# Scattering the expert results into the output by accumulation, with the shared part stored ahead or behind

## The chip, the cores and the metric

The kernel runs on one core of a Trainium2 chip. The metric is the device time of one launch in microseconds (us), the median of several runs. Profiles are of one execution; times in them count from the start of its span.

## The reference

The model takes 64 sequences of 64 points with 7 channels. After a signature layer and an attention layer, the last layer is a mixture of experts over all tokens (4096 in the kernel, 32 tiles of 128, 128 features each). What matters here is how the output comes together from three terms:

```python
h = _L0_tok_ref(x, L0_tok_W, L0_tok_b)
h = h + _L0_attn_ref(_layernorm(h), ...)
h = h + _L0_ffn_ref(_layernorm(h), ...)

# _L0_ffn_ref, with E = 8 experts, K = 1 chosen per token, I = 512 hidden
logits = xf @ gate_w.T
wts, idx = jax.lax.top_k(logits, K)
wts = jax.nn.softmax(wts, axis=-1)          # 1.0, since K = 1
h = silu(xf @ w1[e].T) * (xf @ w3[e].T)     # e: the token's expert
y = h @ w2[e].T
y = y + gelu(xf @ sw1.T) @ sw2.T            # the shared part, for all tokens
```

So out = residual + shared part + the part of the token's one expert.

## The kernel before, in words

Tokens lie in 32 tiles; `h` in SBUF holds the residual of all 32 (128 partitions x 32 x 128, 2 MB). A first stage, to about 510 us, loops over the tiles and makes the residual, the normalised rows `x2` and the router's logits; GpSimd scatters the rows of `x2`, with their token number behind them, into `sorted_rows` in DRAM, in order of expert and padded to slabs of 128 (L502).

The shared part is computed in eight groups of four tiles (`GROUPS` = 8, `AHEAD` = 6). SyncE loads a group's columns (`load_group`, L377), ScalarE and VectorE split them in two parts for an exact product (`xg_hi`, `xg_lo`, L709 and L796), TensorE does `up` and `down`, ScalarE the gelu between (L714), and VectorE adds the result to `h` (`add_shared`, L1152, counted by the semaphore `added`). Groups 0 to 5 are done ahead of the experts. Groups 6 and 7 have their up products behind the last slab and their down products at the very end, in PSUM banks 5, 6 and 1, so that TensorE has work while the last transfers land.

Between them run the experts: `SORTED` = 39 slabs. For each slab j, with k = j mod 2, SyncE reads the slab's first row number from `row_i` and loads 128 rows (`load_rows`, L413), when slab j-2 has been transposed and its token numbers kept (`rT_psum`, `id_kept`); TensorE transposes the rows (L1556) and does the two up products, ScalarE silu (L739), VectorE the product of the two (L1204), the copy of the expert's weights (L1190) and the copy of the token numbers (L1199), TensorE the down product, ScalarE copies the result to `y[k]` (L750), and GpSimd scatters `y[k]` to `expert_rows` in DRAM by token number (L573); rows of padding carry a number out of range and are skipped. The copy to `y[k]` waits until the scatter of slab j-2 has landed (`y_sent`).

Behind the experts, SyncE waits for all scatters, reads `expert_rows` back in eight transfers of 256 KB (L432, groups 6 and 7 first), VectorE adds each to `h` (L1233), then adds the last shared results from PSUM to groups 6 and 7 in three pieces (`add_last_shared`, L1239), and SyncE stores the output in nine transfers as the pieces are finished (L437). Each engine's work stands in one program in order; each waits on semaphores counted. SyncE's queue carries all plain transfers, GpSimd's the scatters.

Of the kernel before, what the change touches and what calls it, by code (L numbers as in the profile page):

```python
# [30 lines left out]
F32 = mybir.dt.float32  # L31
# [4 lines left out]
ALU = mybir.AluOpType  # L36
# [3 lines left out]
P = 128  # L40
SEQS, LEN, CHANNELS = 64, 64, 8
TILES = SEQS * LEN // P
DIM = 128
# [22 lines left out]
GROUP = 4  # L66
# [25 lines left out]
def build(nc, x_next, x_prev, w_low, w_high, tok_b, wqkv, u_qkv, wout_t, u_columns, b_out,  # L92
          scalars, gate_t, w13_t, w2_t, sw1_t, sw2_t, square, mask_c, steps, out):
    with ExitStack() as ctx:
# [3 lines left out]
        def sem(name):  # L98
            return ctx.enter_context(nc.semaphore(name))

        x2T_dram = nc.dram_tensor("x2_columns", [P, TILES * P], F32, kind="Internal").ap()
        sorted_rows = nc.dram_tensor("sorted_rows", [SLABS * P, ROW], F32, kind="Internal").ap()
        expert_rows = nc.dram_tensor("expert_rows", [TILES * P, DIM], F32, kind="Internal").ap()

# [163 lines left out]
        rowsT = late(2, P)  # L268
        expert_in = x2[:].rearrange("p t r -> p (t r)")[:, 0:TILES * DIM].rearrange("p (t d) -> p t d", d=DIM)
        w13_tile = x2[:].rearrange("p t r -> p (t r)")[:, 0:4 * HIDDEN].rearrange("p (k i) -> p k i", k=2)  # L270
# [46 lines left out]
        xg_loaded = [sem(f"x_group_loaded{n}") for n in range(2)]  # L317
        expert_loaded = [sem(f"expert_rows_loaded{n}") for n in range(GROUPS)]
        expert_added, finished, out_sent = sem("expert_rows_added"), sem("finished"), sem("out_sent")
        rows_in = [sem(f"rows_in{n}") for n in range(2)]  # L320
# [12 lines left out]
        def _(sp):  # L333
# [42 lines left out]
            def load_group(g):  # L376
                sp.dma_start(xg_in[:, g % 2, :], x2T_dram[:, g * GROUP * P:(g + 1) * GROUP * P]) \  # L377
                    .then_inc(xg_loaded[g % 2], 16)
# [31 lines left out]
            def load_rows(j, k):  # L410

                row = sp.value_load(row_i[0:1, bass.ds(j, 1)], min_val=0, max_val=(SLABS - 1) * P)
                sp.dma_start(rows[:, k, :], sorted_rows[bass.ds(row, P), :]).then_inc(rows_in[k], 16)  # L413

            for g in range(GROUPS - 4):
                sp.wait_ge(xg_lo, g + 3)
                load_group(g + 4)
            sp.wait_ge(pos_ready, 4)
            sp.wait_ge(scattered, 16 * TILES)
            for j in range(2):  # L420
                load_rows(j, j)
            with sp.Fori(2, SORTED - 2, 2) as j:
                for k in range(2):
                    sp.wait_ge(rT_psum, j + (k - 1))
                    sp.wait_ge(id_kept, j + (k - 1))
                    load_rows(j + k, k)
# [3 lines left out]

            def load_experts(g):
                sp.dma_start(expert_in[:, g * GROUP:(g + 1) * GROUP, :],  # L432
                             expert_rows[g * GROUP * P:(g + 1) * GROUP * P, :].rearrange("(t p) d -> p t d", p=P)) \
                    .then_inc(expert_loaded[g], 16)

            def store(first, tiles):
                sp.dma_start(out[first * P:(first + tiles) * P, :].rearrange("(t p) d -> p t d", p=P),  # L437
                             h[:, first:first + tiles, :]).then_inc(out_sent, 16)

            for k in range(2):  # L440
                sp.wait_ge(y_sent[k], 16 * ((SORTED + 1 - k) // 2))
            for g in (AHEAD, AHEAD + 1, *range(AHEAD)):
                load_experts(g)
            for g in range(GROUPS - 1):
                sp.wait_ge(finished, g + 1)
                store(g * GROUP, GROUP)
            for n in range(2):
                sp.wait_ge(finished, GROUPS + n)
                store((GROUPS - 1) * GROUP + 2 * n, 2)
            sp.wait_ge(out_sent, 16 * (GROUPS + 1))  # L450


        @block.gpsimd
        def _(pool):
# [114 lines left out]
            scatter(range(EARLY, TILES))  # L569

            for j in range(SORTED):
                pool.wait_ge(y_done, j + 1)
                nc.gpsimd.indirect_dma_start(  # L573
                    out=expert_rows[:, :], out_offset=bass.IndirectOffsetOnAxis(ap=ids[:, j:j + 1], axis=0),
                    in_=y[:, 2 if j == SORTED - 1 else j % 2, :], in_offset=None, bounds_check=TILES * P - 1, oob_is_err=False) \
                    .then_inc(y_sent[j % 2], 16)

# [202 lines left out]
        def _(d):  # L780
# [448 lines left out]

            def add_experts(g):  # L1230
                d.wait_ge(expert_loaded[g], 16)
                hg = tiles_of(h, g * GROUP, GROUP)
                return V.tensor_tensor(hg, hg, tiles_of(expert_in, g * GROUP, GROUP), ALU.add)  # L1233

            def add_last_shared(n, tiles, bank, done):

                d.wait_ge(down_psum, done)
                hg = tiles_of(h, AHEAD * GROUP + n, tiles)
                V.tensor_tensor(hg, hg, B[bank][:, 0:tiles * DIM], ALU.add).then_inc(finished, 1)  # L1239

            for g in (AHEAD, AHEAD + 1):
                add_experts(g).then_inc(expert_added, 1)
            for g in range(AHEAD):
                add_experts(g).then_inc(finished, 1)
            d.wait_ge(expert_added, 2)
            add_last_shared(0, GROUP, 5, AHEAD + 1)
            add_last_shared(GROUP, 2, 6, AHEAD + 2)
            add_last_shared(GROUP + 2, 2, 1, AHEAD + 3)


# [460 lines left out]
```

## Time and profile before

| | before |
|---|---|
| median of 3 runs | 676.93 us (676.33 to 677.5) |
| the profiled execution | 676.65 us |
| its span | 674.8 us |
| TensorE busy | 638.4 us (95%) |
| VectorE, ScalarE, GpSimd busy | 417.5, 288.2, 298.7 us |
| DMA moved | 61.81 MB, 92 GB/s mean |
| DMA in the last of 40 slices | 250 GB/s |

The span runs from the first to the last instruction that the profile shows. A row of the timeline gives start and duration in us, engine, line, operation, output and input; what stands in brackets is the idle time of the engine ahead of it and what ended it. Names are those of the memory and not always of the view: `prob` stands for `y`, `xvo` for the slab's rows, `x` for the copied expert weights or the reloaded rows, `levels` for w2, `sw` for the shared weights, `tail`, `z`, `xqk` and `xvp` for the gelu's results. SPq rows are transfers issued by SyncE, with the time that the issue took; "to landing" counts from the start of the issue to the completion.

### The profile page before, as it was taken

To read this page: it belongs to the slowest core of one execution; us is meant where nothing else is said; L and a number is where in the kernel's file an instruction comes from. 1 tells how busy PE (TensorE), PEld (TensorE's weight loads), DVE (VectorE), ACT (ScalarE), POOL (GpSimd) and SP (SyncE) were. 2 spreads that over 40 slices of the span, in tenths; PEclk is the share of its full clock that TensorE was granted. 3 is DMA by queue.
4 is the path that set the end of the run, shared out by engine and by line. 5 is a ranking of instruction groups with operands and counts; after the bars stand their busy time and mean duration, and the time that the engine had idled before them with its cause. 6 is when DMAs were issued, how large, how long until landed. Compare 5 with 4: busy or idle time off the path is not lost.

```text
span 674.8 us, 14377 instructions
## 1 busy us (share of the span) xinstructions
PE 638.4 (95%) x4237; PEld 539.0 (80%) x4270; DVE 417.5 (62%) x1073; ACT 288.2 (43%) x656; POOL 298.7 (44%) x336
## 2 busy tenths in 40 slices
PE   5989999999999999999999999999798999999994
PEld 3767888877888788887788887778577999999994
DVE  7966666666666666665666667776535354555534
ACT  3334444544445444445444454433374433444450
POOL 1355444545445454455444454445853213333330
PEclk9989999999999999999999999999988999999997
DMA  8511433534634434334343342112335211111108
GB/s 310 220 68 33 106 78 85 116 80 101 118 78 111 92 87 101 78 92 111 78 105 82 79 114 46 36 35 69 86 91 191 64 33 38 43 44 44 46 26 250
DMA packets 70006, 61.81 MB, mean 92 GB/s; under 512 B 6092, under 2 KB 58189, under 8 KB 69600
## 3 DMA queue, kind: packets, MB, share of 16 engines
q1 hardware_dynamic: 67712, 57.31, 33.6%
q0 software_dynamic: 2272, 4.22, 1.8%
q8 instruction: 13, 0.21, 0.1%
q14 instruction: 9, 0.07, 0.0%
HBM read 18.88 MB, written 26.30 MB: 67 GB/s over the span
## 4 chain that ended last, share of the span: by engine, by line
PE 81%; DVE 7%; issue 4%; POOL 3%; ACT 2%; DMA 1%; SPq 1%; DVEq 0%; POOLq 0%; ACTq 0%
PE bank L1256 74%; PE bank L1312 2%; PE bank L1465 2%; POOL sorted_rows L502 1%; POOL z L487 1%; DMA x<-expert_rows 1%; SPq L432 1%; PE bank L1556 1%; PE bank L1371 1%; PE bank L1362 0%; PE bank L1317 0%; POOL z L489 0%; PE bank L1316 0%; DMA sq<-square 0%; DVE utl L796 0%
## 5 line engine op out<-in xcount | busy, mean ns | idle before, releaser
L1256 PE MATMUL bank<-whigh,uth 128*128 128x512 f32 x512 | 168.8, 410 | 1.2 <-DVE lowt L796 1.2
L1256 PEld LDWEIGHTS bank<-whigh,uth 128*128 128x128 f32 x512 | 92.2, 190 | 28.0 <-issue 7.4
L1256 PE MATMUL bank<-whigh,utl 128*128 128x512 f32 x256 | 101.8, 398 | 0.0
L496 POOL TENSOR_TENSOR rstd<-rstd,powers 128x1 f32<-128x1 f32 x64 | 35.3, 551 | 119.9 <-DVE rstd L889 64.7
L487 POOL TENSOR_TENSOR z<-z 128x512 f32<-128x512 f32 x32 | 42.3, 1322 | 91.0 <-DVE z L902 91.0
L573 POOL DMA_INDIRECT expert_rows<-prob,ids x39 | 38.3, 983 | 89.2 <-ACT prob L750 89.2
L1256 PE MATMUL bank<-xvo,x 128*128 128x128 f32 x624 | 76.4, 276 | 0.7 <-issue 0.4
L1256 PEld LDWEIGHTS bank<-xvo,x 128*128 128x128 f32 x624 | 72.8, 192 | 1.4 <-issue 0.7
L1256 PE MATMUL bank<-xT,qkw 128*128 128x128 f32 x512 | 63.7, 278 | 0.0
L1256 PEld LDWEIGHTS bank<-xT,qkw 128*128 128x128 f32 x512 | 60.8, 195 | 0.1
L1256 PEld LDWEIGHTS bank<-whigh,utl 128*128 128x128 f32 x256 | 48.3, 189 | 11.9
L902 DVE TENSOR_TENSOR z<-bank,v 128x512 f32<-128x512 f32 x64 | 44.2, 691 | 20.6 <-PE bank L1256 16.8
L1204 DVE TENSOR_TENSOR z<-tail,bank 128x512 f32<-128x512 f32 x39 | 26.8, 688 | 48.3 <-PE bank L1256 48.3
L641 ACT ACTIVATE prob<-prob 128x512 f32<-128x512 f32 x32 | 20.2, 633 | 66.4 <-DVE prob L1020 63.6
L623 ACT ACTIVATE xqk<-bank,fac 128x512 f32<-128x512 f32 x64 | 43.9, 690 | 7.2 <-PE bank L1256 5.7
L651 ACT COPY pt<-bank 128x512 f32<-128x512 f32 x32 | 18.8, 587 | 63.8 <-PE bank L1465 61.7
L1256 PEld LDWEIGHTS bank<-xvp,pt 128*64 128x64 f32 x512 | 30.1, 137 | 18.2 <-issue 18.2
L482 POOL TENSOR_TENSOR e3l<-e,e3h 128x512 fp32r<-128x512 f32 x31 | 40.4, 1304 | 7.8 <-DVE xn L923 6.5
L1256 PE MATMUL bank<-vow,xTh 128*128 128x512 f32 x128 | 43.1, 418 | 0.0
L911 DVE TENSOR_TENSOR h<-bank,tokb 128x128 f32<-128x128 f32 x32 | 9.3, 291 | 54.2 <-PE bank L1256 54.2
L1256 PE MATMUL bank<-xqk,xT 128*64 128x512 f32 x128 | 34.5, 618 | 8.5 <-DVE logits L957 4.2
L630 ACT COPY xvo<-bank 128x512 f32<-128x512 f32 x64 | 37.6, 587 | 10.6 <-PE bank L1256 8.9
(229 smaller groups left out, 1325.9 us busy)
## 6 DMA issues: line engine op xcount, KB each, us to landing
sorted_rows<-blank SPq DMA_DIRECT2D x24, 709.5 KB, 6.3
xvp<-xvo SPq DMA_DIRECT2D x128, 128.0 KB
w<-w_t SPq DMA_DIRECT2D x1, 4096.0 KB, 12.0
xvo<-sorted_rows SPq DMA_DIRECT2D x39, 64.5 KB, 1.9
w<-w_high SPq DMA_DIRECT2D x4, 512.0 KB, 6.8
x_columns<-x2t SPq DMA_DIRECT2D x32, 64.0 KB
xg_in<-x_columns SPq DMA_DIRECT2D x8, 256.0 KB
levels<-w_t SPq DMA_DIRECT2D x1, 2048.0 KB, 7.7
```

Source lines behind the costliest of these rows:

```text
L482: G.tensor_tensor(e3l[:], e3[:], e3h[:].bitcast(F32), ALU.subtract).then_inc(e3_lo, 1)
L487: G.tensor_tensor(z4[:], z[:, 0:4, :], z[:, 4:8, :], ALU.add).then_inc(tree, 1)
L496: G.tensor_tensor(rstd[:, n, 1:2], rstd[:, n, 0:1], powers[:, 0:1], ALU.pow) \
L573: nc.gpsimd.indirect_dma_start(out=expert_rows[:, :], out_offset=bass.IndirectOffsetOnAxis(ap=ids[:, j:j + 1], axis=0), in_=y[:, 2 if j == ...
L623: A.activation(xqk[:, :, 4 * n:4 * n + 4, :], B[5 + n][:].rearrange("p (s h k) -> p s h k", s=2, h=4), ACT.Copy, scale=fac[:, 1:2]).then_i ...
L630: A.copy(xvo[:, n, :, :].rearrange("p c d -> p (c d)"), B[7 - 2 * n][:]) \
L641: A.activation(prob[:], prob[:], ACT.Exp).then_inc(exp_done, 1)
L651: A.copy(pt[:].rearrange("k c s q -> k (c s q)"), B[6][:]).then_inc(pT_sb, 1)
L902: V.tensor_tensor(z[:, cs, :], B[1 + half][:].rearrange("p (c d) -> p c d", c=4), spread(v[:, bass.ds(s, 1), cs].rearrange("p o c -> p (o ...
L1204: V.tensor_tensor(hidT[:, k, :, :].rearrange("p c t -> p (c t)"), act[:, k, :], B[2 + 2 * k][:], ALU.mult).then_inc(hid_done, 1)
L1256: return T.matmul(out_, lhsT, rhs, start=start, stop=stop)
L1312: T.transpose(B[0][:, col(c)], u4[:, col(c)], ident)
```

## The change

The tensor `expert_rows` is gone. GpSimd's 39 scatters go to `out` itself and add to what is there (`compute_op=ALU.add`). For that the rest of the output must be there first: SyncE stores the residual of groups 6 and 7 when it is complete (`h2_done`), and each of groups 0 to 5 when its shared part has been added, all counted by `out_begun`, between the loads of the columns (L377) and between the first row loads (L413). GpSimd waits for all eight before its first scatter. Behind the experts only groups 6 and 7 are read back, as sums of residual and expert part; VectorE adds the last shared results to these in three pieces and writes `h`, and SyncE stores the three pieces.

```diff
-        expert_rows = nc.dram_tensor("expert_rows", [TILES * P, DIM], F32, kind="Internal").ap()
...
+            def out_tiles(first, tiles):
+                return out[first * P:(first + tiles) * P, :].rearrange("(t p) d -> p t d", p=P)
+
+            def store(first, tiles, done):
+                sp.dma_start(out_tiles(first, tiles), h[:, first:first + tiles, :]).then_inc(done, 16)
+
+            sp.wait_ge(h2_done, TILES)
+            for g in range(AHEAD, GROUPS):
+                store(g * GROUP, GROUP, out_begun)
             for g in range(GROUPS - 4):
                 sp.wait_ge(xg_lo, g + 3)
                 load_group(g + 4)
+                sp.wait_ge(added, g + 1)
+                store(g * GROUP, GROUP, out_begun)
             sp.wait_ge(pos_ready, 4)
             sp.wait_ge(scattered, 16 * TILES)
             for j in range(2):
                 load_rows(j, j)
-            with sp.Fori(2, SORTED - 2, 2) as j:
+            sp.wait_ge(added, AHEAD - 1)
+            store((AHEAD - 2) * GROUP, GROUP, out_begun)
+            for j in range(2, 4):
+                sp.wait_ge(rT_psum, j - 1)
+                sp.wait_ge(id_kept, j - 1)
+                load_rows(j, j % 2)
+            sp.wait_ge(added, AHEAD)
+            store((AHEAD - 1) * GROUP, GROUP, out_begun)
+            with sp.Fori(4, SORTED - 2, 2) as j:
...
             for k in range(2):
                 sp.wait_ge(y_sent[k], 16 * ((SORTED + 1 - k) // 2))
-            for g in (AHEAD, AHEAD + 1, *range(AHEAD)):
-                load_experts(g)
-            for g in range(GROUPS - 1):
-                sp.wait_ge(finished, g + 1)
-                store(g * GROUP, GROUP)
             for n in range(2):
-                sp.wait_ge(finished, GROUPS + n)
-                store((GROUPS - 1) * GROUP + 2 * n, 2)
-            sp.wait_ge(out_sent, 16 * (GROUPS + 1))
+                sp.dma_start(sums_in[:, n * GROUP:(n + 1) * GROUP, :], out_tiles((AHEAD + n) * GROUP, GROUP)) \
+                    .then_inc(sums_loaded[n], 16)
+            sp.wait_ge(finished, 1)
+            store(AHEAD * GROUP, GROUP, out_sent)
+            for n in range(2):
+                sp.wait_ge(finished, 2 + n)
+                store((GROUPS - 1) * GROUP + 2 * n, 2, out_sent)
+            sp.wait_ge(out_sent, 16 * 3)
...
+            pool.wait_ge(out_begun, 16 * GROUPS)
             for j in range(SORTED):
                 pool.wait_ge(y_done, j + 1)
                 nc.gpsimd.indirect_dma_start(
-                    out=expert_rows[:, :], out_offset=bass.IndirectOffsetOnAxis(ap=ids[:, j:j + 1], axis=0),
-                    in_=y[:, 2 if j == SORTED - 1 else j % 2, :], in_offset=None, bounds_check=TILES * P - 1, oob_is_err=False) \
-                    .then_inc(y_sent[j % 2], 16)
+                    out=out[:, :], out_offset=bass.IndirectOffsetOnAxis(ap=ids[:, j:j + 1], axis=0),
+                    in_=y[:, 2 if j == SORTED - 1 else j % 2, :], in_offset=None, bounds_check=TILES * P - 1, oob_is_err=False,
+                    compute_op=ALU.add).then_inc(y_sent[j % 2], 16)
...
-            def add_experts(g):
-                d.wait_ge(expert_loaded[g], 16)
-                hg = tiles_of(h, g * GROUP, GROUP)
-                return V.tensor_tensor(hg, hg, tiles_of(expert_in, g * GROUP, GROUP), ALU.add)
-
             def add_last_shared(n, tiles, bank, done):
 
                 d.wait_ge(down_psum, done)
-                hg = tiles_of(h, AHEAD * GROUP + n, tiles)
-                V.tensor_tensor(hg, hg, B[bank][:, 0:tiles * DIM], ALU.add).then_inc(finished, 1)
-
-            for g in (AHEAD, AHEAD + 1):
-                add_experts(g).then_inc(expert_added, 1)
-            for g in range(AHEAD):
-                add_experts(g).then_inc(finished, 1)
-            d.wait_ge(expert_added, 2)
+                V.tensor_tensor(tiles_of(h, AHEAD * GROUP + n, tiles), tiles_of(sums_in, n, tiles),
+                                B[bank][:, 0:tiles * DIM], ALU.add).then_inc(finished, 1)
+
+            d.wait_ge(sums_loaded[0], 16)
             add_last_shared(0, GROUP, 5, AHEAD + 1)
+            d.wait_ge(sums_loaded[1], 16)
             add_last_shared(GROUP, 2, 6, AHEAD + 2)
             add_last_shared(GROUP + 2, 2, 1, AHEAD + 3)
```

## Rows read from the trace of the kernel before

**Rows 1.** Chain of work that ended last, 640 to 675 us: start, us, what

```profile
656.11 2.11 DMA expert_rows<-prob,ids
658.23 0.39 SPq L432
...
663.37 4.94 DMA x<-expert_rows
```

**Rows 2.** Timeline of the tail: TensorE, VectorE, SyncE

```profile
661.08 0.69 DVE L1233 TENSOR_TENSOR h<-h,x 128x512 f32<-128x512 f32 x1 [8.71 <-DMA x<-expert_rows]
...
661.89 0.61 PE L1256 MATMUL bank<-sw,z 128*128 128x128 f32 x4
...
665.46 0.61 PE L1256 MATMUL bank<-sw,xvp 128*128 128x128 f32 x4
...
669.87 0.41 DVE L1239 TENSOR_TENSOR h<-h,bank 128x256 f32<-128x256 f32 x1
...
670.71 0.59 SPq L437 DMA_DIRECT2D out<-h  x1
```

**Rows 3.** Landing of the nine output stores (L437), and SyncE's end (L94)

```profile
DMA to landing us min/median/max: 3.1/3.2/3.7
...
L94 SPq COMPARE_BRANCH  x1: 38/38/38, 674.4 to 674.4; - x1
```

**Rows 4.** Landing of the 39 scatters of expert results (L573)

```profile
DMA to landing us min/median/max: 2.1/2.6/3.4
```

**Rows 5.** DMA issues: kind, count, KB each, median us to landing (a slab's row load)

```profile
xvo<-sorted_rows SPq DMA_DIRECT2D x39, 64.5 KB, 1.9
```

**Rows 6.** Timeline of 505 to 550 us, SyncE, ScalarE, VectorE, TensorE and GpSimd

```profile
509.64 0.34 SPq L374 DMA_DIRECT2D x_columns<-x2t  x1
510.02 0.43 SPq L407 DMA_DIRECT2D levels<-w_t  x1
511.20 0.34 SPq L377 DMA_DIRECT2D xg_in<-x_columns  x1
...
518.33 0.62 ACT L709 CAST uth<-xg_in 128x512 fp32r<-128x512 f32 x1 [2.10 <-DMA xg_in<-x_columns]
520.52 1.29 ACT L714 ACTIVATE xqk<-bank 128x512 f32<-128x512 f32 x2 [1.57 <-PE bank L1256]
...
525.91 0.48 PE L1256 MATMUL bank<-uth,sw 128*128 128x512 f32 x1
...
528.78 0.60 PE L1256 MATMUL bank<-sw,xqk 128*128 128x128 f32 x4
...
529.49 0.69 DVE L1152 TENSOR_TENSOR h<-h,bank 128x512 f32 x1 [3.78 <-remote]
...
531.94 0.35 SPq L413 DMA_DIRECT2D xvo<-sorted_rows  x1
...
533.07 0.35 SPq L413 DMA_DIRECT2D xvo<-sorted_rows  x1
...
533.57 0.68 DVE L1152 TENSOR_TENSOR h<-h,bank 128x512 f32 x1
...
538.71 0.38 PE L1556 MATMUL bank<-sq,xvo 128*128 128x128 f32 x2
...
541.17 2.05 PE L1256 MATMUL bank<-xvo,x 128*128 128x128 f32 x16 [0.29 <-DVE x L1190]
...
545.05 0.69 DVE L1152 TENSOR_TENSOR h<-h,bank 128x512 f32<-128x512 f32 x1 [0.26 <-PE bank L1256]
...
548.89 1.00 POOL L573 DMA_INDIRECT expert_rows<-prob,ids  x1 [19.38 <-ACT prob L750]
```

**Rows 7.** Timeline of two slabs in the steady state: ScalarE's result, GpSimd's scatter

```profile
635.89 0.27 ACT L750 COPY prob<-bank 128x128 f32<-128x128 f32 x1 [0.63 <-PE bank L1256]
...
636.92 0.98 POOL L573 DMA_INDIRECT expert_rows<-prob,ids  x1 [1.73 <-ACT prob L750]
...
641.46 0.27 ACT L750 COPY prob<-bank 128x128 f32<-128x128 f32 x1 [0.62 <-PE bank L1256]
```

## What I predict, and from what

> **What bounds the kernel now.** I read the chain of waits first, since a change behind the experts pays only where that chain runs, then the timeline of the last 20 us by engine, then the landings of the transfers, and last the stretch from 505 to 550 us, where the moved stores go. Through the router, the shared groups and the 39 expert slabs the chain is TensorE's. It leaves TensorE at the last slab: the last scatter is issued at 656.11 and lands 2.11 us later, SyncE issues eight reloads of the expert rows from 658.23, the last of them at 663.37, and that one counts as landed 4.94 us later [rows 1]. Only then can VectorE finish: the adds of the last shared groups end at 669.87 + 0.41 = 670.28, SyncE issues the last store at 670.71, and it has landed when SyncE goes on at 674.4 [rows 2, 3]. TensorE had finished the last product that these adds need at 665.46 + 0.61 = 666.07 [rows 2]. So 4.2 us of VectorE's last add, and more behind it, are owed to 2 MB of reloads and 2 MB of stores, not to arithmetic. The reader is to see in rows 1 and 2 that the end is a transfer chain laid over a TensorE chain that ends 4 us earlier.
>
> **Tail, the gain.** The change takes out six of the eight reloads, the eight adds of 128x512, and six of the nine stores there. What is left I follow from the last scatter.
> The scatter is now an accumulation: each row of 512 B of the output is read, added to and written. No row of before shows one. It can't be quicker than a plain scatter, since the same bytes still travel the same way: 2.1 us at least, 2.6 median, 3.4 at most [rows 4]. The dear end is a read followed by a plain scatter, one after the other: 1.9 (a slab's row load, [rows 5]) + 2.6 = 4.5 us. I take 3.2, nearer the plain scatter, because the 64 KB are the same, and the read may overlap within the transfer.
> Landing at 656.11 + 3.2 = 659.3; reload of group 6 issued at 659.4 and landed 2.85 us later, as the first of the eight was (issued 658.23, add begun 661.08, [rows 1, 2]): 662.2. TensorE ends group 6 at 661.89 + 0.61 = 662.5 [rows 2], so the reload is already covered. Group 7's reload is issued half a us later and is there at some 663.2, while its second half comes from TensorE at 666.07. Even with the dear 4.5 us it is there at 664.6. So the accumulation's price in the tail is nothing; it would show from a landing of about 6 us on.
> VectorE's last add then starts right behind TensorE and takes 0.41: 666.1 + 0.4 = 666.5; SyncE issues the store of 128 KB at 666.6. Its landing: the nine stores of before took 3.1 to 3.7 us [rows 3], with up to eight others in the queue. The other bound is the last spill of 64 KB in the same 512 B rows: issued at 509.64, and SyncE was past the wait for it when it issued the load at 511.20, so at most 1.56 us [rows 6]. With one store of 128 KB two us ahead of it the last one is alone; I take 2.6, between the ends. It lands at 669.2, and 674.8 - 674.4 = 0.4 us of ending follow: span 669.6, a gain of 5.2. With 1.56 it is 668.6, with 3.7 it is 670.7.
> [...]
>
> **Expert stage, where the accumulation can cost.** ScalarE writes y of slab j only when slab j-2's scatter has landed. In the steady state the result is copied at 635.89 for 0.27 us, its scatter starts at 636.92, and the copy two slabs on is at 641.46 [rows 7]. So a scatter may take 641.46 - 636.92 = 4.54 us before ScalarE waits; the plain one took 3.4 at most. Above 4.5 the loop of two slabs (5.57 us) is paced by the landing, and with 37 slabs behind it each us more costs 18.5 us. At 3.2 it costs nothing: TensorE's 2.8 us a slab cover it. The dear end from the rows, 4.5, lies just at the edge. GpSimd's own instruction, 0.98 us in a slab of 2.79, may take up to 2.5 us before it binds. More descriptors should lengthen it somewhat; I count nothing.
> The Trainium skill (Collectives: The Full Stack, The bandwidth ceiling) says that a reducing transfer is slowed by its second source read and not by the add, and measures about half the rate of a copy. No run here shows that yet. It would leave a scatter of 64 KB far under the 4.5 us and the sum as it is.
>
> **Stores moved ahead.** SyncE gets eight stores of 256 KB, at 0.38 us of issue each, and three kinds of neighbours.
> First, groups 6 and 7 are stored before the load of columns of group 4, which was issued at 511.20 behind the 2 MB load of w2 [rows 6]. That load had ScalarE wait until 518.33. Two issues are 0.8 us and 512 KB in the queue; at the 284 GB/s at which the 2.36 MB before that point passed (510.02 to 518.33) they are 1.8 us, so the columns are there at 520.2 and copied at 520.8. ScalarE's next gelus, which started at 520.52, start 0.3 us late; TensorE wants their product only in the down product that starts at 528.78 [rows 6]. Cost nothing.
> Second, the loads of groups 5 to 7 now stand behind a wait for the previous group's add as well. The last of these, group 3's add, runs at 533.57 + 0.68 = 534.25 [rows 6]. Behind it on SyncE are a store (0.4) and the first two row loads, which were issued at 531.94 and 533.07. With 0.8 us to read the row number they go out at 535.5 and 536.6, 3.6 us later, and land at 537.4 and 538.5 by the median 1.9 [rows 5, 6]. TensorE transposes them at 538.71 [rows 6]. That is on the edge: with the largest neighbouring landing, 3.7, TensorE would wait 1.7 us, of which 0.29 are slack before the first expert product at 541.17 [rows 6]. I take 0.1 us.
> Third, stores of groups 4 and 5. The first goes out at about 539.8, before the next row load. The second goes out when VectorE's add at 545.05 is done, 545.8, and lands by 549.5 at the latest. GpSimd now waits for all eight stores before its first scatter; that was at 548.89 [rows 6]. Likely nothing, at most 0.7 us + 0.5 of preparation, and the second scatter at 551.7 absorbs it. This wait is right by the Trainium skill (DMA: Bandwidth & Descriptors, Rules for kernel authors): a plain write beside an accumulation of the same bytes is lost; no run here shows that.
> Sum: 674.8 - 5.2 + 0.1 = 669.7 us of span, a run of 676.65 - 5.1 = 671.55 in the profiled execution's own count. The median of the three runs is 0.28 above the profiled one, so 671.8.
>
> **Rivals.**
> (a) The accumulation paces the experts: slower. Its landing decides, from 4.5 us on. At 4.54 + 5.1 / 18.5 = 4.82 the whole gain is gone; at 5.5 the kernel takes 671.8 + 18.5 x 0.96 = 690 us, at 6 us 699. For it: no row of an accumulation exists, and eight rows per engine with a read before each write need not overlap as well as plain writes. Against it: even a serial read and write come to 4.5. Chance 0.15 for slower (above 678.3), 0.04 for the narrow band of no change (675.6 to 678.3).
> (b) The moved transfers hold up TensorE between 510 and 550: row loads landing late (up to 1.4 us, above), and a code fetch. For the latter: VectorE stood 3.78 us until 529.49 for something that the profile calls remote, though the product it needed was done when TensorE began the next group at 525.91, 0.3 us of overlap aside [rows 6]. If that is code coming through the same DMA engines, 512 KB of stores before it add up to 2 us, and only the part of it beyond TensorE's own lead is lost. Together 1 to 3 us of the gain go: 672.8 to 674.8. Chance 0.14.
> (c) The change doesn't shorten the tail by as much, since the last store lands as slowly as now (3.7) and no less: 672.9 at most; that is the upper end of my own forecast and no sign of its own. Against more: TensorE's end at 666.07 is untouched.
> (d) A quicker end, with a lone store of 1.6 us or less: 670.7. Part of the forecast, its outer edge (below 670.4) 0.05.
>
> **How the numbers follow.** Forecast with its edges (670.4 to 672.9): 0.62; (b) 0.14; (d) beyond the edge 0.05; (a) 0.15 slower and 0.04 same. The likeliest time is 671.8. The range must hold 8 in 10: from 670.4 to 675.0 holds 0.76, so I reach into the narrow band about no change, to 677.0, which holds 0.80. About 0.2% (1.35 us) is what a measurement of this kernel can tell from none. Faster 0.81, same 0.04, slower 0.15.
>
> **What would show it.** After: the scatter's landing (right if 2.6 to 4.5 and ScalarE nowhere waits for one; the loop stays at 2.79 us a slab); TensorE's last product still 10 to 11 us behind the last scatter's issue; VectorE's last add within 0.5 us of it; only two reloads; the last store's landing 1.6 to 3.1 and not 3.7; the first two row loads at 535.5 and 536.6 and no wait of TensorE before 538.7; the first scatter near 549. A slab period above 2.9 us would prove (a), a shift of the first expert product with an unchanged period (b).

## The result and the profile after

The changed kernel takes 670.04 us (median of four runs, 669.5 to 671.37), the kernel before 676.63 beside it: a ratio of 0.9905 with a 95% interval of 0.9886 to 0.9925, so 5 to 8 us less. In a second set it took 669.38 us against 676.4, ratio 0.989 (0.9873 to 0.9907). The forecast was 671.8 and its range began at 670.4: the direction and the place were right, the size was too small, and the first median fell 0.4 us below the range.

The profiled execution has a span of 668.4 us (670.26 us as a run). First its page: GpSimd's busy time has grown by 22.5 us, and each of its scatters from 0.98 to 1.56 us, while TensorE's busy time is nearly what it was (638.4 and 637.1 us).

```profile
span 668.4 us, 14362 instructions
PE 637.1 (95%) x4237; PEld 538.7 (81%) x4270; DVE 411.8 (62%) x1065; ACT 289.3 (43%) x656; POOL 321.2 (48%) x336
L583 POOL DMA_INDIRECT out<-prob,ids x39 | 60.9, 1560 | 65.9 <-ACT prob L760 65.9
```

The end of its chain of waits (start, us, what) answers [rows 1]. The transfers have left the chain: TensorE runs without a stop to the last product, then comes one add.

```profile
648.57 17.22 PE bank L1258 x128
665.78 0.02 issue
665.81 0.42 DVE h L1243
```

The timeline of the tail answers [rows 2 and 3]: last scatter, two reloads (658.51 and half a us later), TensorE's last product, the three adds, the last store, and the moment when SyncE has seen it land.

```profile
655.78 1.56 POOL L583 DMA_INDIRECT out<-prob,ids  x1 [1.00 <-ACT prob L760]
...
658.51 0.94 SPq L452 DMA_DIRECT2D x<-out  x2
...
662.30 0.69 DVE L1243 TENSOR_TENSOR h<-x,bank 128x512 f32<-128x512 f32 x1 [10.26 <-PE bank L1258]
...
664.09 0.42 DVE L1243 TENSOR_TENSOR h<-x,bank 128x256 f32<-128x256 f32 x1 [1.10 <-PE bank L1258]
...
665.16 0.61 PE L1258 MATMUL bank<-sw,xvp 128*128 128x128 f32 x4
665.81 0.42 DVE L1243 TENSOR_TENSOR h<-x,bank 128x256 f32<-128x256 f32 x1 [1.29 <-PE bank L1258]
...
666.25 0.37 SPq L418 DMA_DIRECT2D out<-h  x1
...
L94 SPq COMPARE_BRANCH  x1: 38/38/38, 668.0 to 668.0; - x1
```

All three adds are released by TensorE and none by a reload, as the brackets say. The last product ends at 665.16 + 0.61 = 665.77, so 2.6 us are left behind TensorE (8.7 before: 674.8 - 666.07). The list of transfers (count, KB each, median us to landing) shows what the sum had as guesses: an accumulating scatter lands in 3.3 us, a store of 128 KB in 1.8, and the two reloads take 3.0 and 4.3 (3.7 is their median). The last scatter was quicker than the others: SyncE, which waits for it, issued the reloads 658.51 - 655.78 = 2.73 us after its start.

```profile
out<-prob,ids POOLq DMA_INDIRECT x39, 3.3
...
x<-out SPq DMA_DIRECT2D x2, 256.0 KB, 3.7
...
out<-h SPq DMA_DIRECT2D x2, 128.0 KB, 1.8
```

In the stretch ahead of the experts, answering [rows 6], the first shared up product of group 2 started at 512.07 instead of 510.99. By that much the executions differ before they reach anything that was changed. All later times are therefore to be read from that point.

```profile
520.95 0.62 ACT L719 CAST uth<-xg_in 128x512 fp32r<-128x512 f32 x1 [3.60 <-DMA xg_in<-x_columns]
521.62 1.29 ACT L724 ACTIVATE xqk<-bank 128x512 f32<-128x512 f32 x2
...
527.41 0.69 DVE L1162 TENSOR_TENSOR h<-h,bank 128x512 f32 x1 [0.60 <-PE bank L1258]
...
536.00 1.51 SPq L412 DMA_DIRECT2D xvo<-sorted_rows  x2
...
540.62 0.68 PE L1258 MATMUL bank<-sw,xqk 128*128 128x128 f32 x4 [0.43 <-issue]
...
542.48 1.95 PE L1258 MATMUL bank<-xvo,x 128*128 128x128 f32 x16
...
550.17 1.61 POOL L583 DMA_INDIRECT out<-prob,ids  x1 [19.55 <-ACT prob L760]
```

### The profile page after: what moved, and what is told of

Its sections match the earlier page's. It is cut to its first block, busy times and chain, and to the rows that moved or that the text cites. A ratio compares the mean times of both kernels' runs of the same rounds, so it can differ in the third digit from the quotient of the medians.

```text
span 668.4 us, 14362 instructions
## 1 busy us (share of the span) xinstructions
PE 637.1 (95%) x4237; PEld 538.7 (81%) x4270; DVE 411.8 (62%) x1065; ACT 289.3 (43%) x656; POOL 321.2 (48%) x336
## 3 DMA queue, kind: packets, MB, share of 16 engines
q0 software_dynamic: 6640, 4.22, 4.6%
## 4 chain that ended last, share of the span: by engine, by line
PE 84%; DVE 6%; POOL 5%; issue 3%; ACT 1%; DMA 0%; SPq 0%; ACTq 0%; DVEq 0%; POOLq 0%
PE bank L1258 78%; POOL sorted_rows L511 3%; PE bank L1314 2%; PE bank L1467 2%; POOL z L496 1%; PE bank L1558 1%; POOL rstd L505 1%; PE bank L1373 1%; PE bank L1364 1%; PE bank L1319 0%; POOL z L498 0%; PE bank L1318 0%; DMA sq<-square 0%; DVE utl L806 0%; DVE whigh L806 0%
## 5 line engine op out<-in xcount | busy, mean ns | idle before, releaser
L583 POOL DMA_INDIRECT out<-prob,ids x39 | 60.9, 1560 | 65.9 <-ACT prob L760 65.9
## 6 DMA issues: line engine op xcount, KB each, us to landing
xvo<-sorted_rows SPq DMA_DIRECT2D x39, 64.5 KB, 1.8
```

What stands on the lines that cost most here:

```text
L583: nc.gpsimd.indirect_dma_start(out=out[:, :], out_offset=bass.IndirectOffsetOnAxis(ap=ids[:, j:j + 1], axis=0), in_=y[:, 2 if j == SORTED ...
```

## The experiments

I read three stretches in every profile, since the executions differ by up to 3 us before the first changed instruction: (A) from the first up product of shared group 2 to the first expert product, (B) from there to the end of TensorE's last product, (C) from there to the end of the span. Each is a difference of two times in the timeline, as for the kernel after: 542.48 - 512.07 = 30.41, 665.77 - 542.48 = 123.29, 668.4 - 665.77 = 2.63. What is left, the start up to group 2, is nothing of the change's. The two kernels with one buffer, whose slab loop runs at another pace, are not in the table.

| kernel | A | B | C | stops in slabs 6 and 10 |
|---|---|---|---|---|
| before | 30.18 | 124.90 | 8.73 | 1.24 |
| before, second profile | 30.21 | 125.05 | 8.45 | 1.35 |
| before, third | 30.17 | 125.38 | 8.57 | 1.79 |
| before, fourth | 30.00 | 124.36 | 8.48 | 0.68 |
| before + early stores | 30.56 | 124.38 | 8.96 | 0.90 |
| the same, second profile | 30.38 | 125.22 | 8.78 | 1.63 |
| the same, third | 30.32 | 124.37 | 8.46 | 0.86 |
| plain scatter, no early stores | 30.24 | 124.15 | 2.62 | 0.58 |
| the same, second profile | 30.01 | 124.28 | 2.66 | 0.54 |
| after | 30.41 | 123.29 | 2.63 | 0.00 |
| after, second profile | 30.37 | 123.51 | 2.65 | 0.00 |
| plain scatter | 30.40 | 123.70 | 2.71 | 0.00 |
| reload all | 30.38 | 123.55 | 9.49 | 0.00 |
| small last piece | 30.41 | 124.16 | 2.34 | 0.69 |
| the same, second profile | 30.37 | 123.31 | 2.30 | 0.00 |
| late reload | 28.98 | 123.42 | 3.55 | 0.13 |

The last column is how far the distances between VectorE's products of slabs 6 and 7 and of slabs 10 and 11 exceed the usual 2.79 us, in sum.

**Plain scatter.** Is the accumulation covered?

```diff
-                    in_=y[:, 2 if j == SORTED - 1 else j % 2, :], in_offset=None, bounds_check=TILES * P - 1, oob_is_err=False,
-                    compute_op=ALU.add).then_inc(y_sent[j % 2], 16)
+                    in_=y[:, 2 if j == SORTED - 1 else j % 2, :], in_offset=None, bounds_check=TILES * P - 1, oob_is_err=False).then_inc(y_sent[j % 2], 16)
```

> The changed kernel with the 39 scatters as plain writes (the output lacks the shared part and residual where an expert row overwrote it). My theory: the accumulation is hidden behind TensorE, so the time is that of the changed kernel, 670.0 us, within 0.5; the scatter lands in 2.6 us instead of 3.3 and GpSimd's instruction falls from 1.56 to 0.98 us. The rival, that the longer scatter costs something in the slab loop, expects 1 to 3 us less than the changed kernel and a shorter slab period than 2.79.

669.49 us, ratio 0.9908 (0.9889 to 0.9926), no different from the changed kernel. Its scatters land in 2.5 us and take GpSimd 0.98:

```profile
L583 POOL DMA_INDIRECT out<-prob,ids x39: 982/982/1002, 548.4 to 654.4; - x39
DMA to landing us min/median/max: 2.1/2.5/4.2
```

So accumulation adds 0.8 us to the median landing, 0.58 of it GpSimd's own work on the instruction, and in this kernel it costs nothing that the times show.

**No early stores.** What do the moved stores cost? All eight and GpSimd's wait are left out, on top of the plain scatter.

```diff
-            sp.wait_ge(h2_done, TILES)
-            for g in range(AHEAD, GROUPS):
-                store(g * GROUP, GROUP, out_begun)
...
-                sp.wait_ge(added, g + 1)
-                store(g * GROUP, GROUP, out_begun)
...
-            pool.wait_ge(out_begun, 16 * GROUPS)
```

> As the plain scatter, and with the eight stores ahead of the experts and GpSimd's wait for them left out (the output holds the expert part alone in groups 0 to 5). My theory: the stores cost TensorE 0.1 to 0.3 us between 510 and 541 us, so this is within 0.4 us of the plain scatter, about 669.8. The rival, that the moved stores hold up the stretch before the experts, expects 1 to 2 us less, 668 to 669, with the first up product of the shared groups and the first expert product earlier.

669.86 us, ratio 0.9914 (0.9893 to 0.9934): no difference. Stretch A puts the stores at 0.2 to 0.3 us: 30.0 to 30.2 in the six profiles without them, 30.3 to 30.6 in nine with them (in the tenth, the late reload's, TensorE's first products of group 2 took 0.50 instead of 0.80 us, and the granted clock was 1.00 (2.4 GHz) from 511 to 513 us where the changed kernel had 0.50 (1.2 GHz), so A can't be compared). With the stores TensorE pauses 0.40 to 0.61 us behind the transposition of the first rows in the five profiles read for it (0.43 in the row at 540.62 above); without them it pauses there not at all and 0.30 before the first expert product, for VectorE's copy of the weights:

```profile
541.63 2.05 PE L1247 MATMUL bank<-xvo,x 128*128 128x128 f32 x16 [0.30 <-DVE x L1189]
```

The rival that the moved transfers cost 1 to 3 us is out.

**Reload all.** Is the whole gain in the tail? The changed kernel with all eight groups reloaded, added and stored behind the experts, in the order of before.

```diff
-            for n in range(2):
-                sp.dma_start(sums_in[:, n * GROUP:(n + 1) * GROUP, :], out_tiles((AHEAD + n) * GROUP, GROUP)) \
-                    .then_inc(sums_loaded[n], 16)
+            for g in (AHEAD, AHEAD + 1, *range(AHEAD)):
+                sp.dma_start(sums_in[:, g * GROUP:(g + 1) * GROUP, :], out_tiles(g * GROUP, GROUP)) \
+                    .then_inc(sums_loaded[g], 16)
...
+            for g in (AHEAD, AHEAD + 1):
+                add_experts(g).then_inc(expert_added, 1)
+            for g in range(AHEAD):
+                add_experts(g).then_inc(finished, 1)
```

> The changed kernel up to the last scatter, with the tail of the kernel before: eight reloads, eight adds, nine stores (the shared part is counted twice). My theory: the whole gain is in the tail, so this takes what the kernel before takes, 676.6 us within 0.7, with 8.5 to 9 us from TensorE's last product to the end, and stores that land in 3.1 to 3.7 us. The rival, that 1.6 us of the gain lie in the slab loop, expects 675.0 and a slab stage of 123.3 us from the first expert product to TensorE's end, as against 124.9 in the kernel before.

675.22 us, ratio 0.9989 (0.9976 to 1.0003). Putting the old tail back gives back all but at most 1.6 us of the gain. Stretch C is 9.5 us and the stores wait in the queue again: the seven of 256 KB at the end take 2.8 to 3.6 us, the two of 128 KB 2.8 and 3.7 (1.8 in the changed kernel). The 15 stores of the first row are these seven and the eight early ones.

```profile
out<-h SPq DMA_DIRECT2D x15, 256.0 KB, 3.3
...
x<-out SPq DMA_DIRECT2D x8, 256.0 KB, 4.8
...
out<-h SPq DMA_DIRECT2D x2, 128.0 KB, 3.3
```

But stretch B is 123.55 here. So B is not something that the tail's transfers did; the expectation's rival (675.0 us, B 123.3) was right.

**One buffer.** What is a landing worth once it is on the path? ScalarE's result goes to one buffer instead of two, so it waits for the scatter of the slab just before. The same edit in both kernels:

```diff
-                    in_=y[:, 2 if j == SORTED - 1 else j % 2, :], in_offset=None, bounds_check=TILES * P - 1, oob_is_err=False,
+                    in_=y[:, 2 if j == SORTED - 1 else 0, :], in_offset=None, bounds_check=TILES * P - 1, oob_is_err=False,
...
-                if reused:
-                    a.wait_ge(y_sent[k], (j - k) * 8)
-                nc.scalar.copy(y[:, 2 if is_tile(j, SORTED - 1) else k, :], B[5 + k][:, 0:DIM]).then_inc(y_done, 1)
+                if not is_tile(j, 0) and not is_tile(j, SORTED - 1):
+                    a.wait_ge(y_sent[1 - k], (j + k) * 8)
+                nc.scalar.copy(y[:, 2 if is_tile(j, SORTED - 1) else 0, :], B[5 + k][:, 0:DIM]).then_inc(y_done, 1)
```

> The changed kernel with one buffer for the expert result instead of two, so that ScalarE waits for the scatter of the slab just before. It measures what a landing costs once it paces the loop. My theory: a slab then takes copy 0.27 + 0.77 to the scatter's start + landing 3.3 + 0.05 = 4.4 us instead of 2.79, in 36 slabs 58 us more, 728 us in all. The rival, that a landing on the path is quicker or slower than in the covered loop (fewer transfers beside it, or rows that don't overlap), expects a slab period off 4.4 by 0.5 us or more.

> The kernel before with one buffer for the expert result, against the same edit of the changed kernel. My theory: the plain scatter's landing (2.6 us in the covered loop) paces the loop: 0.27 + 0.77 + 2.6 + 0.05 = 3.7 us a slab, 33 us more than before, 709 us. The difference to the other kernel, 0.7 us a slab, is then what accumulation costs where nothing covers it. The rival, that the uncovered costs are alike, expects a period of 4.3.

The changed kernel takes 727.53 us with it, the kernel before 693.07 (one run each; the difference is far above the spread of 2 us). ScalarE's rows of the first and then of the second show two results, each released by a scatter's landing:

```profile
601.87 0.27 ACT L760 COPY prob<-bank 128x128 f32<-128x128 f32 x1 [3.41 <-DMA out<-prob,ids]
...
606.27 0.27 ACT L760 COPY prob<-bank 128x128 f32<-128x128 f32 x1 [3.48 <-DMA out<-prob,ids]
```

```profile
602.15 0.27 ACT L750 COPY prob<-bank 128x128 f32<-128x128 f32 x1 [2.38 <-DMA expert_rows<-prob,ids]
...
605.45 0.27 ACT L750 COPY prob<-bank 128x128 f32<-128x128 f32 x1 [2.24 <-DMA expert_rows<-prob,ids]
```

A slab takes 4.40 and 3.30 us. The formula of the prediction (copy 0.27, 0.77 to the scatter's start, the landing, 0.05) holds with the landings of these runs: 3.4 gives 4.5, and 2.2 gives 3.3. My expected 3.7 for the plain one was wrong because I took the landing of the covered loop, 2.6. Part of that is the load of a slab's rows: in the covered loop one was under way beside 35 of the 39 plain scatters, which landed in 2.6 at the median, and the last four, with none, landed in 2.1; with one buffer only 4 of the 39 plain scatters had a load beside the part behind GpSimd's, and 30 of the accumulating ones. So uncovered, the accumulating version costs 1.1 us more per slab, but not all of that is shown to be the accumulation. With no row load beside them the last three accumulating scatters of the changed kernel landed in 2.7, 0.6 later than the plain ones, which is what GpSimd's instruction is longer by.

The two buffers and TensorE's 2.79 us per slab are what makes it free, and the margin was thinner than the median says. Two of ScalarE's results are put down to a landing just at the limit of 4.54 us, the first of them this one:

```profile
555.74 1.56 POOL L583 DMA_INDIRECT out<-prob,ids  x1 [1.26 <-ACT prob L760]
...
560.27 0.27 ACT L760 COPY prob<-bank 128x128 f32<-128x128 f32 x1 [0.70 <-DMA out<-prob,ids]
```

From the start of this scatter to ScalarE's copy two slabs on are 4.53 us, and 4.57 for the other (566.89 to 571.46). By the events in the trace three of the 39 scatters landed in 4.3 to 4.5 us, and each had a 16 KB transfer of the queue that the page calls `instruction` beside it (below). The view's own maximum of 3.4 leaves them out, because it has a landing for 19 of the 39 only. TensorE lost nothing by them: the slabs stay at 2.79 us.

**Late reload.** How much cover is left in the tail? The reloads are issued only when TensorE has ended group 6's down product.

```diff
+            sp.wait_ge(down_psum, AHEAD + 1)
             for n in range(2):
```

> The changed kernel with the reloads of groups 6 and 7 issued only when TensorE has ended group 6's down product, 3.7 us later than now. It measures how much of the reload TensorE covers. My theory: group 7's reload, 4.3 us to landing, then comes 1.2 us behind TensorE's last product, and two adds of 0.42 follow instead of one: 4.3 to 4.5 us from TensorE's end to the end of the span instead of 2.6, so 1.8 us more. The rival, that a reload with a quiet queue lands in 2.9 us, expects only 0.4 us more.

669.12 us, ratio 0.9897 (0.9879 to 0.9915): the runs can't tell it from the changed kernel, but stretch C grew from 2.6 to 3.55 us. The three adds now stand in a row behind the reload and no longer behind TensorE, whose last product ended at 662.95:

```profile
662.41 1.55 DVE L1244 TENSOR_TENSOR h<-x,bank 128x512 f32<-128x512 f32 x3 [13.19 <-DMA x<-out]
```

The issue was 3.5 us ahead of TensorE's end, as against 7.3 in the changed kernel. The reloads landed in 2.9 and 3.3 us, where 3.0 and 4.3 were measured in the changed kernel, so group 7's was there 0.2 us behind TensorE and not 1.2. The result, 0.9 us more, lies between theory (1.8) and rival (0.4). It also shows the cover: 3.8 us of delay cost 0.9, so a landing of the last scatter up to some 3 us later would have cost nothing.

**Small last piece.** Can what is left be cut? The last piece of two tiles becomes two of one, the last in a bank of its own.

```diff
-            last_down(AHEAD + 1, 1, range(2, GROUP), 1)
+            last_down(AHEAD + 1, 1, range(2, GROUP - 1), 1)
+            last_down(AHEAD + 1, 1, range(GROUP - 1, GROUP), 2)
...
-            add_last_shared(GROUP + 2, 2, 1, AHEAD + 3)
+            add_last_shared(GROUP + 2, 1, 1, AHEAD + 3)
+            add_last_shared(GROUP + 3, 1, 2, AHEAD + 4)
```

> The changed kernel with its last piece of two tiles cut in two of one tile, the last in a PSUM bank of its own: one add and one store more. What is left behind TensorE is add, store issue, landing and end, 2.6 us. My theory: the add shrinks from 0.42 to 0.28 and the 64 KB land in 1.6 instead of 1.8, so 0.3 us less, 669.7. The rival, that the additional issue on the store queue is late and takes it back, expects no difference or 0.3 us more.

> The changed kernel, unchanged, beside the kernel before and the next one on one chip. My theory: 6.0 us less than the kernel before (5.5 to 6.6), of which 6.1 are the tail and -0.2 the stores ahead. From its first shared up product to its first expert product 30.4 us, as against 30.2 without the stores; from TensorE's end to the end of the span 2.6.

> The version with a last piece of one tile, beside the changed kernel on one chip. Its profile had 2.34 us behind TensorE's end, as against 2.63. My theory: 0.3 us less than the changed kernel. The rival: no difference that five rounds can show.

Both of its profiles have 2.3 us behind TensorE instead of 2.6, as the smaller add (0.29 for 0.42) and the quicker landing (1.5 for 1.8) say. The times are 669.51 and 669.83, the changed kernel's beside the second 669.38, ratio 0.9896 (0.9877 to 0.9914) against 0.989. 0.3 us is below what these runs resolve; the version isn't shown to be faster. The changed kernel itself missed its second expectation: 7.0 us less than the kernel before it, where 5.5 to 6.6 were expected. The tail and the stores were as expected; the rest is stretch B.

**Where 1.5 us of stretch B went.** The kernel before, and the kernel before with the eight early stores alone (groups stored again at the end; the places of the later ones are as in the change):

```diff
+            sp.wait_ge(h2_done, TILES)
+            for g in range(AHEAD, GROUPS):
+                early_store(g * GROUP, GROUP)
             for g in range(GROUPS - 4):
                 sp.wait_ge(xg_lo, g + 3)
                 load_group(g + 4)
+                sp.wait_ge(added, g + 1)
+                early_store(g * GROUP, GROUP)
...
```

> The kernel before, unchanged, profiled once more. In the first profile it took 124.9 us from the first expert product to TensorE's end; five profiles of kernels with the same slab loop took 123.3 to 124.2. My theory: this part varies by about a us from execution to execution (short stops of TensorE, mostly at the ends of the unrolled loop) and the change has no part in it, so a second profile of the kernel before gives 123.3 to 124.9, more likely below 124.5. The rival, that the change itself shortens the slab loop by 1 us or more, expects 124.9 again.

> The kernel before with one part of the change alone: the eight stores ahead of the experts, at the changed kernel's places on the queue (the output is stored again at the end, as before). Open is why TensorE needs 124.9 and 125.1 us from the first expert product to its end in two profiles of the kernel before, and 123.3 to 123.6 in four of six with the stores. The difference lies in two slabs of the first pass of the unrolled loop, the sixth and the tenth (3.1 to 3.8 us instead of 2.79). Theory one, the stores on the queue (and the row loads written out between them) remove those stops: 123.3 to 123.8 us here, 0.2 more ahead, 1.0 less in all than the kernel before. Theory two, it is the new scatter or the shorter program behind the loop: 124.9 us here, and 0.2 us more than the kernel before in all.

> A second profile of the kernel with plain scatters and without the eight stores, whose first one had 3.07 and 3.09 us in the sixth and the tenth slab. If the stores remove the stops, it has both again, 0.5 to 1.3 us together. If the stops are chance, it may have none. From the first shared up product to the first expert product it takes 30.2 us, unless TensorE's clock comes up sooner.

> The kernel before once more, for the stops in the sixth and the tenth slab (so far 1.2 and 1.3 us together). If the stops belong to a program without the stores, 0.5 to 1.4 us again; if they are chance, it may have none.

> The kernel before with the eight early stores alone, once more. Its first profile had no stop in the sixth slab and 0.9 us in the tenth. Theory one, the stores remove stops: 0 to 0.9 us, on average 0.3, and the time 0.3 to 0.8 us below the kernel before. Theory two, chance: the same stops as the kernel before on average, and the time 0.2 us above.

> The kernel before once more, as the third. Timed against itself it is to show no difference, within 0.1%.

> As the kernel before with the eight early stores alone, a third profile, the same expectations.

The kernel before had B at 124.4 to 125.4 in four profiles, the changed one at 123.3 and 123.5. My expectation for the second profile of before (at most 124.9) missed: it was 125.05. Timed against itself, the kernel before gives ratios of 0.9995 (0.9986 to 1.0003) and 0.9997 (0.9985 to 1.001). The kernel with the early stores alone has 124.4, 125.2 and 124.4, and takes 675.77, 675.77 and 675.45 us, ratios 0.9992 (0.9982 to 1.0001), 0.999 (0.9978 to 1.0003) and 0.9997 (0.9984 to 1.0011): the stores alone don't remove the stops, and they don't cost anything that can be measured either. The stops stand in the first pass of the unrolled slab loop; later pauses are 0.2 us at most. In the chain of waits of the kernel before they look like this: a transposition takes 0.20 us in the chain instead of 0.11, and 24 products take 3.24 us instead of 2.68, with a gap of 0.19 for nothing that the profile shows.

```profile
557.95 0.20 PE bank L1556
558.15 1.03 PE bank L1256 x8
559.18 0.19 issue
559.38 2.02 PE bank L1256 x16
```

In the same slab of the second profile of before the idle time is put down to a late row load ahead of the transposition:

```profile
559.01 0.14 PEld L1556 LDWEIGHTS bank<-sq,xvo 128*128 128x128 f32 x1 [0.33 <-DMA xvo<-sorted_rows]
```

That row load is the cause. It was issued at 555.04 in the kernel before and at 556.19 in the changed one, and these are the times to its landing, the first for before and the second for after:

```profile
DMA to landing us min/median/max: 2.7/2.7/2.7
...
DMA to landing us min/median/max: 1.9/1.9/1.9
```

What made it late is in the trace too. The page counts a queue of its own for instructions, and the trace holds its packets:

```profile
q8 instruction: 13, 0.21, 0.1%
```

One of these 13 transfers of 16 KB ran from 555.45 to 556.67. Of the 128 packets of the row load 120 had ended by 556.55, and the last eight ended behind it, up to 557.20. The two loads in question (for the seventh and the eleventh slab), in all 16 profiles of the table, divide without an exception:

| 16 KB instruction transfer starts after the load's issue by | load lands in | stop | cases |
|---|---|---|---|
| 0.1 to 1.0 us | 2.2 to 3.1 us | 0.13 to 1.01 us | 18 |
| 1.3 to 2.2 us | 1.7 to 1.9 us | none | 14 |

A stop is as long as the landing exceeds some 2.1 us. So the stops are instruction transfers that fall on a row load. In the two profiles of the changed kernel they came later and fell on a scatter instead, which the two buffers cover. What sets their time stays open. It isn't the accumulation alone: the plain scatter has no such stops, and without the early stores it has them again, 0.58 and 0.54 us (the latter run took 669.94). So neither the stores alone nor the new scatter alone takes them away, and in the small last piece they came once and not the other time. They depend on the program, and within one program on the execution, so a gain in B is not one to count on.

## Why the prediction was right, and where not

The direction and the mechanism came out as forecast. Two terms of the sum failed, both too dear: the landing of the last store (2.6 us, measured 1.8), and the slab loop, whose change was put at nothing without a look at its first pass (measured 1.6 us less in the profile, 1.5 over all profiles).

- **The place of the gain: right.** The end was a chain of transfers laid over a TensorE chain that ended earlier. Now TensorE's last product releases the last add, and putting the old tail back takes the gain back.
- **Accumulation in the tail and in the slabs: right.** Landing 3.2 forecast, 3.3 measured at the median and 2.7 for the last, and covered: of ScalarE's 39 results two have their idle time (0.70 and 0.73 us) put down to a landing, which is at most 0.03 more than the 0.70 that it stands for TensorE in every second slab anyway. The dear end of 4.5 was reached three times (4.3 to 4.5), not by a serial read and write but beside an instruction transfer; rival (a) was nearer than the median says. The pace formula behind rival (a) was confirmed to 0.1 us by the one-buffer kernels; its condition didn't occur.
- **GpSimd's instruction: counted at no change, grew by 0.58 us.** It lies in 1.7 us of idle time per slab and costs nothing.
- **Reload: mis-sized, covered all the same.** 2.85 forecast, 3.0 to 4.3 measured. Group 6's was there at 661.5, 0.7 us before TensorE ended its product at 662.20, and the bracket of the first add names TensorE. Group 7's was there at 663.3, 2.5 us before TensorE's end, so by my estimate the accumulation would have shown in the tail from a landing of 2.7 + 2.5 = 5.2 us on, and not of 6.
- **Last store: the term that was mis-sized.** 2.6 forecast, 1.8 measured. I went to the middle between a queued store (3.1 to 3.7) and a spill of 64 KB alone (1.56), though by my own sum the last store was alone. The nearer row was the spill. With an add 0.04 us behind TensorE, stretch C came to 2.6 instead of the 3.5 forecast: 0.9 us.
- **Stores moved ahead: 0.1 forecast, 0.2 measured.** Read from the same start (1.08 us off all times), the columns of group 4 came at 519.9, where 520.2 was forecast. The first row load went out at 534.9, where 535.5 was forecast, and the first scatter at 549.1, as forecast.
- **VectorE's unexplained wait of 3.78 us** was not there in the changed kernel (0.60 behind TensorE at 527.41), and in the three other profiles of before it is 0.61 to 0.62 as well. So it was no property of the stretch, and rival (b) had nothing to add to. What it was stays open. Code did come beside the data transfers, as (b) supposed, but where it cost something it delayed row loads in the slab loop, in the kernel before more than in the changed one.
- **Missing from the sum: the stops of stretch B,** 1.24 us in the profile of before and none in the changed one. No step of mine looked at the slab loop's period over all slabs; I took the steady 2.79 us as the whole of it. In the kernel before two row loads of the first pass landed late beside instruction transfers (2.7 us each instead of 1.8 to 1.9); in the changed kernel none did. That was luck for the change as far as is known, and no merit of it.

Forecast 669.7, measured 668.4 in the profile: -0.9 in the tail, +0.1 ahead, +1.1 before anything changed, -1.6 in B, which makes -1.3. Over all profiles the change is worth 5.9 us in the tail (8.56 mean to 2.64), 0.2 us ahead the other way, and 1.5 us in B (124.9 mean to 123.4), 7.2 in sum, for measured medians that differ by 6.6 and 7.0 us. The 0.4 us by which the time fell out of the range are thus the store's landing and B together: the tail alone (0.9 us) would have left it inside, B alone (1.5) at its edge, which lay 1.4 below the forecast. Two small slips of the working changed nothing: by its own rows group 7's reload is there at 662.8, or 664.1 at the dear end, and not at 663.2 and 664.6, and the range up to 677.0 takes in a part only of the band of 0.04 (675.6 to 678.3), so it held somewhat less than 0.80.

## What to carry to other kernels

When a change empties a queue, take the landing of a transfer from a row with an empty queue, not from the rows that stand in the place of the removed ones. Work that is only there to merge results (reload, add, store) can be given to accumulating scatters, if their landing has a slot of buffering and a covering engine: ask for the limit (here 4.54 us by two buffers) before asking for the price. And sum a loop's period over all its passes before calling it steady; here the first pass held 0.7 to 1.8 us of stops. Where one transfer of many lands late, look for a packet of the instruction queue beside it.

## What the runs showed of the hardware

- An accumulating scatter of 128 rows of 512 B takes GpSimd 1.56 us and lands in 3.3 us from its start; the plain one 0.98 and 2.5. From the end of GpSimd's part the two land nearly alike, in 1.7 and 1.5 us, so the second read adds little to a landing. It isn't free for the DMA engines: queue 0 has 6640 packets instead of the plain scatter's 2272 for the same 4.22 MB, and they take 4.6% of the 16 engines' span instead of 1.8. The rule of half the rate (the Trainium skill, Collectives: The Full Stack, The bandwidth ceiling) can be neither seen nor refuted by the landings at this size.
- A landing depends more on what is queued than on its size: alone a store of 64 KB landed in 1.5 us, of 128 KB in 1.8 and of 256 KB in 2.2, and one of 128 KB behind seven and eight others in 2.8 and 3.7; a plain scatter landed in 2.1 us with no row load beside it and 2.6 with one.
- One transfer of 16 KB on the instruction queue had a row load of 64.5 KB land in 2.2 to 3.1 us instead of 1.7 to 1.9 when it started within 1.0 us of the load's issue (18 of 18 cases), and an accumulating scatter beside one landed in 4.1 to 4.5 us instead of 3.3 (three in each profile of the changed kernel).
- The Trainium skill has a fit for transfers that GpSimd issues (DMA: Bandwidth & Descriptors, Anatomy of one DMA), 2.0 us plus the bytes over 436 GB/s. For 128 KB that makes an estimate of 2.3 us. The last store of 128 KB, which SyncE issued, took 1.8, so the fit is not to be carried over to that queue.
